# A decoder layer on one core: feed-forward weights prepared in the last pairs of the self-attention, the cross attention's end in halves and pairs of tiles

## The reference

```python
x = layernorm(x + self_attention(x))     # 16 heads of 64, rotary, causal
x = layernorm(x + cross_attention(x))    # 16 heads of 16, 5 samples a query
x = layernorm(x + feed_forward(x))       # 704 hidden units, fake quantisation
```

## Time and profile before

| engine | busy us | share |
|---|---|---|
| TensorE, matmuls | 1846.8 | 88% |
| VectorE | 1521.4 | 72% |
| GpSimd | 1496.5 | 71% |
| ScalarE | 1316.2 | 62% |

### The profile page before, as it was taken

The page is one execution under the profiler, slowest core; times in us unless marked ns, Lnnn a source line. Parts: engine busy times, 40 slices in busy tenths (PEclk is TensorE's granted clock), DMA queues, the critical chain, the costliest instruction groups (busy, mean ns, idle before and its releaser), DMA issues. The chain is left out here.

```text
span 2110.7 us, 43268 instructions
## 1 busy us (share of the span) xinstructions
PE 1846.8 (88%) x17255; PEld 1127.7 (53%) x17259; DVE 1521.4 (72%) x2147; ACT 1316.2 (62%) x1802; POOL 1496.5 (71%) x1122
## 2 busy tenths in 40 slices
PE   5889999999999999999999999588889898884475
PEld 3545455555555555555455454466677677663333
DVE  6857867868878868878768764257667676777787
ACT  3546656656556656666656655057887877874287
POOL 0767868878868878868778777168768797757256
PEclk8989999999999999999999999679999999997698
DMA  7022122122132032132032020200000000100002
GB/s 226 27 51 66 46 71 66 40 57 66 41 76 66 16 81 66 26 91 66 17 81 66 16 66 27 62 7 8 3 2 8 2 2 2 46 2 2 2 1 80
DMA packets 57511, 92.39 MB, mean 44 GB/s; under 512 B 25312, under 2 KB 35552, under 8 KB 53344
## 3 DMA queue, kind: packets, MB, share of 16 engines
q1 hardware_dynamic: 48096, 89.36, 16.4%
q10 hardware_dynamic: 9216, 0.27, 0.2%
HBM read 51.33 MB, written 4.46 MB: 26 GB/s over the span
## 5 line engine op out<-in xcount | busy, mean ns | idle before, releaser
L947 POOL TENSOR_TENSOR acc<-acc,probs 128x1024 f32<-128x1024 f32 (+3 forms) x320 | 583.0, 1822 | 105.9 <-ACT probs L650 75.4
L650 ACT ACTIVATE probs<-psum 128x1024 f32<-128x1024 f32 (+3 forms) x384 | 290.7, 812 | 162.7 <-PE psum L501 160.7
L594 ACT ACTIVATE chunks<-psum 128x1024 bf16<-128x1024 f32 x288 | 282.0, 1026 | 123.7 <-PE psum L460 78.0
L493 PE MATMUL psum<-operands 64*128 64x512 f32 (+3 forms) x1536 | 309.9, 515 | 17.4 <-ACT chunks L594 16.9
L1523 ACT ACTIVATE onehot<-psum 128x1024 bf16<-128x1024 f32 x320 | 324.5, 1045 | 0.0
L801 DVE TENSOR_REDUCE lows<-chunks 128x2 f32<-128x1024 bf16 (+1 forms) x224 | 266.7, 1217 | 73.4 <-ACT chunks L594 63.5
L517 PE MATMUL psum<-probs,vals 128*64 128x512 f32 (+3 forms) x1536 | 296.1, 503 | 22.5 <-POOL probs L926 12.0
L1353 PE MATMUL psum<-pieces,onehot 128*128 128x64 bf16 x7680 | 281.6, 197 | 14.3 <-ACT vs L1530 13.0
L1353 PEld LDWEIGHTS psum<-pieces,onehot 128*128 128x128 bf16 x7680 | 262.8, 101 | 47.8 <-issue 24.6
L926 POOL TENSOR_SCALAR_AFFINE_SELECT probs<-probs 128x256 f32<-128x256 f32 x256 | 149.2, 600 | 127.5 <-ACT probs L650 127.5
L1994 POOL TENSOR_TENSOR vs<-vs,wgt 128x1280 f32<-128x1280 f32 x64 | 151.9, 2373 | 107.1 <-DVE wgt L1770 102.4
(11 more groups left out here) (243 smaller groups left out, 3397.9 us busy)
## 6 DMA issues: line engine op xcount, KB each, us to landing
operands<-turned SPq DMA_DIRECT2D x124, 256.0 KB, 5.1
rden<-inverse_rows SPq DMA_DIRECT2D x64, 256.0 KB, 3.9
raw<-in_wqk SPq DMA_DIRECT2D x30, 256.0 KB, 4.3
y<-in_x SPq DMA_DIRECT2D x1, 4096.0 KB, 17.9
wo<-in_wo SPq DMA_DIRECT2D x16, 256.0 KB, 2.6
out<-res SPq DMA_DIRECT2D x16, 256.0 KB, 2.1
raw<-in_wv SPq DMA_DIRECT2D x15, 256.0 KB, 4.3
raw<-in_xT SPq DMA_DIRECT2D x12, 256.0 KB, 4.0
```

The costliest lines, as they stand in the source:

```text
L493: nc.tensor.matmul(dst[:, hh, 0:width], ops[n % OBUF][rows, 1, kt * P:(kt + 1) * P].bitcast(F32), ops[n % OBUF][rows, 0, a:a + width].bitc ...
L594: nc.scalar.activation(chunks[k % MBUF][:, :, :], slot("max", n, c)[:, :, :], ACT.Copy, scale=-1.0)\
L650: nc.scalar.activation(probs[u % PBUF][:, :, 0:width], slot("s", n, u)[:, :, 0:width], ACT.Exp, scale=1.0 / D ** 0.5).then_inc(s_exp, 1)
L947: G.tensor_tensor(dst, dst, src, ALU.add).then_inc(s_acc, 1)
```

## The change

It does four things.
1. SyncE loads the raw weights of the feed-forward near the end of the self-attention, into the room of the projection's buffers. In pairs 29 to 31 VectorE takes scales (`PREPARE_AT`) and clips, ScalarE does the scaling (`SCALE_AT`), TensorE transposes in three otherwise empty full slots (`TURN_WEIGHTS_AT`), ScalarE copies. The quantising and the transposes after the last head are removed, and with them the transposed row of w_down's scales; the feed-forward reads the column by DMA instead.
2. In the cross attention the softmax is split in two parts, after the multiplies of units 0 and 1 of the same head, `weights` comes after the multiply of unit 0, and `exps` after unit 2. The last round's softmax is done in two halves of two heads, the first inside heads 62 and 63. GpSimd normalises batch 2 before it weighs round 14, and it leaves head 63's values to VectorE (`weigh_last`).
3. The end works on pairs of tiles: the transposes and copies of the first half of the context ride in heads 13 and 14 of the last batch, the projections with this half are made ahead for six tiles, then transposes, copy, projection, residual and statistics go by pairs, deviations and normalising by halves. The maxima of y are taken batch by batch (`TOP_AT`, `largest`), the last ones here and not in the feed-forward.
4. In the second pair of the self-attention, one `turn` of GpSimd comes after the first masks and additions of that pair.

```diff
+WEIGHTS = 3
+TURN_WEIGHTS_AT = {(PAIRS - 2, 3): 0, (PAIRS - 1, 1): 1, (PAIRS - 1, 3): 2}
+PREPARE_AT = {(PAIRS - 3, 5): [("scales", 0)], (PAIRS - 2, 0): [("scales", 1)], (PAIRS - 2, 2): [("clip", 0)],
+              (PAIRS - 2, 3): [("scales", 2)], (PAIRS - 2, 5): [("clip", 1)], (PAIRS - 1, 1): [("clip", 2)]}
+SCALE_AT = {(PAIRS - 2, 1): 0, (PAIRS - 2, 4): 1, (PAIRS - 1, 0): 2}
...
+    full = ("w", TURN_WEIGHTS_AT[n, m], 0) if (n, m) in TURN_WEIGHTS_AT else full_at(n, m)
...
+            def load_weights():
+                sp.wait_ge(s_split, len(pieces))
+                sp.wait_ge(s_qk_done, QK_UNITS * GROUPS)
...
+                if i == GROUPS - 2:
+                    load_weights()
...
+            def turn_weights(n):
...
+                pe.wait_ge(s_whq, n + 1)
+                wait_slot(pe, "w", n, 0)
...
+            def scale_weights(n):
+                act.wait_ge(s_set, 8)
+                act.wait_ge(s_winv, n + 1)
+                for t in range(IT if n < 2 else KT):
+                    last = nc.scalar.activation(weights.raw[n][:, t, :], weights.raw[n][:, t, :], ACT.Identity,
+                                                bias=magic[:, 0:1], scale=hidden.winv[n][:, t:t + 1])
+                last.then_inc(s_wsc, 1)
...
+            def copy_weights(n):
+                act.wait_ge(s_wht, n + 1)
+                src = slot("w", n, 0).bitcast(BF16)
+                if n < 2:
+                    nc.scalar.activation(hidden.wT[n][:, :, :], src[:, :, 0:INNER], ACT.Copy).then_inc(s_whc, 1)
...
+            def weight_scales(n):
+                wscale, winv = hidden.wscale[n], hidden.winv[n]
+                dve.wait_ge(s_wraw[n], 16 * (3 if n < 2 else 1))
+                V.tensor_reduce(wscale[:, :], weights.raw[n][:, :, :], AX.X, ALU.max, apply_absolute_value=True)\
+                 .then_inc(s_wscale, 1)
+                dve.wait_ge(s_wscale, 2 * n + 1)
+                V.tensor_scalar(wscale[:, :], wscale[:, :], 1.0 / QMAX, None, ALU.mult).then_inc(s_wscale, 1)
+                dve.wait_ge(s_wscale, 2 * n + 2)
+                V.reciprocal(winv[:, :], wscale[:, :]).then_inc(s_winv, 1)
+            def clip_weights(n):
+                dve.wait_ge(s_wsc, n + 1)
+                V.tensor_scalar(weights.quantised[n][:, :, :], whole(weights.raw[n][:, :, :]), QMAX, -QMAX - 1.0,
+                                ALU.min, ALU.max).then_inc(s_whq, 1)
...
-                    if full and full[0] == "qk" and (n or m != LAST_CHUNKS):
+                    elif n == 1 and m == 0:
+                        turn(1, QK_UNITS - 1)
+                    elif full and full[0] == "qk" and (n or m != LAST_CHUNKS):
                         turn(full[1], full[2])
...
+LATE_RIDERS_AT = {(13, 1): ("cT", 0), (13, 3): ("cT", 1), (14, 1): ("cT", 2), (14, 3): ("cT", 3)}
+TOP_AT = {(LATE - 1, 5, 1): 0, (LATE, 10, 0): 1}
...
+            def late_turn(tp):
+                pe.wait_ge(s_c2, NHG * XB)
+                if tp >= 2:
+                    pe.wait_ge(s_c2T, count("cT", LATE, TILE_PAIRS + tp - 2))
+                for t in range(2):
+                    last = nc.tensor.transpose(turn_banks[tp % 2][:, t, :], ctx2[:, 2 * tp + t, (KT - 1) * P:], ident[:, :])
+                last.then_inc(s_c2t, 1)
+            def late_out(t, kt):
+                return nc.tensor.matmul(late[t], outT[:, kt, t * P:(t + 1) * P], wo[:, kt, :],
+                                        start=kt == 0, stop=kt == KT - 1)
+            def late_project(tp):
+                pe.wait_ge(s_c2T, count("cT", LATE, TILE_PAIRS + tp))
+                if 2 * tp >= len(early):
+                    pe.wait_ge(s_done, RIDERS["out"] * LATE + 1)
+                for t in (2 * tp, 2 * tp + 1):
+                    if t >= len(early):
+                        late_out(t, 0)
+                    last = late_out(t, 1)
+                last.then_inc(s_wo, 1)
...
+                    if u == EXPS_AT and j == SOFT_AT and r:
+                        exps(r - 1)
+                    if u == EXPS_AT and n == HEADS_ALL - LAST:
+                        exps(ROUNDS - 1)
+            exps(ROUNDS)
+            for tp in range(TILE_PAIRS):
+                copy_late(tp)
...
+            def late_residual(tp):
+                dve.wait_ge(s_x1b, BIAS_PARTS * XB)
+                dve.wait_ge(s_wo, RIDERS["out"] * LATE + tp + 1)
+                src = psum[:, 2 * tp:2 * tp + 2, 0:E] if 2 * tp < len(early) else psum[:, 0:2, E:2 * E]
+                pair = y[:, LATE * TT + 2 * tp:LATE * TT + 2 * tp + 2, :]
+                V.tensor_tensor(pair, src, pair, ALU.add).then_inc(s_done, 1)
+                dve.wait_ge(s_done, RIDERS["out"] * LATE + tp + 1)
...
+            def weigh_last():
+                j = HG - 1
+                dve.wait_ge(s_vc, UNITS * HEADS_ALL)
+                dve.wait_ge(s_w, len(turns))
+                both = vs[:, (ROUNDS - 1) % 2, j, :, :]
+                v = both.rearrange("p t (k d) -> p (t k) d", d=HD)
+                w = wgt[:, j * TT:(j + 1) * TT, :, :].rearrange("p t k c -> p (t k c)").unsqueeze(2)
+                V.tensor_tensor(v, v, w.broadcast_to([P, TT * NK * 2, HD]), ALU.mult).then_inc(s_wl, 1)
+                dve.wait_ge(s_wl, 1)
+                V.tensor_reduce(ctx2[:, :, (H - 1) * HD:H * HD], both.rearrange("p t (k d) -> p t d k", d=HD), AX.X, ALU.add)
             def gather(r, j):
...
+                    x = ROUNDS - 1 if n >= HEADS_ALL - LAST else r - 1
+                    first = LAST if n >= HEADS_ALL - LAST else SOFT_AT
+                    if x >= 0 and (j, u) == (first, 0):
+                        softmax_scores(x)
+                    if x >= 0 and (j, u) == (first, 1):
+                        softmax_max(x)
+                    if x >= 0 and (j, u) == (first + 1, 0):
+                        weights(x)
                     between(b, h, u)
...
-            softmax(ROUNDS - 1)
-            weights(ROUNDS - 1)
-            dve.wait_ge(s_sam, UNITS * HEADS_ALL)
-            for n, first in enumerate((0, 1, 3)):
-                quantise(n)
-                for j in range(first, (1, 3, HG)[n]):
-                    gather(ROUNDS - 1, j)
+            softmax_scores(ROUNDS)
+            softmax_max(ROUNDS)
+            weights(ROUNDS)
+            gather(ROUNDS - 2, HG - 1)
+            for j in range(LAST):
+                gather(ROUNDS - 1, j)
+            weigh_last()
+            gather(ROUNDS - 1, LAST)
             dve.wait_ge(s_x2, XB - 1)
-            st.then(V.tensor_reduce(hidden.ytop[:, 0:1], y[:, 0:(XB - 1) * TT, :], AX.XY, ALU.max,
-                                    apply_absolute_value=True))
-            for t in range(TT):
-                residual(XB - 1, t)
-                if t % 4 == 3:
-                    x2_statistics(XB - 1, range(t - 3, t + 1))
-            aggregate(1, s_var2)
-            x2_normalise(XB - 1, range(TT))
+            largest(XB - 2, (XB - 2) * TT, (XB - 1) * TT)
+            for tp in range(TILE_PAIRS):
+                late_residual(tp)
+                statistics(LATE, range(2 * tp, 2 * tp + 2))
+                if tp % 2:
+                    aggregate(1, s_var2, range(2 * tp - 2, 2 * tp + 2))
+            for half in range(2):
+                x2_normalise(half)
+                first = LATE * TT + TT // 2 * half
+                largest(LATE + half, first, first + TT // 2)
             st.settle()
         @block.gpsimd
@@ -1958,11 +2130,11 @@
                 pool.wait_ge(s_dev1, 1)
                 G.tensor_tensor(rstd[0][:, :], rstd[0][:, :], power[:, :], ALU.pow).then_inc(s_std1, 1)
-            def x2_deviations(b):
-                pool.wait_ge(s_var2, b + 1)
...
+                if b == LATE:
+                    x2_deviations(b - 1)
+                    x2_normalise(b - 1)
                 weigh_values(NHG * b + 2)
-                if b:
+                if 0 < b < LATE:
                     x2_deviations(b - 1)
                     x2_normalise(b - 1)
             weigh_values(ROUNDS - 1)
-            x2_deviations(XB - 1)
+            weigh_values(ROUNDS, HG - 1)
+            for half in range(2):
+                x2_deviations(LATE + half, slice(TT // 2 * half, TT // 2 * (half + 1)))
```

320 lines of the change are left out of this document (184 added, 136 removed).

## The result

The changed kernel takes 2099.33 us (median of 20 runs, 2092.98 to 2103.79) against 2109.28 for the kernel before (20 runs, 2100.65 to 2113.27): a ratio of 0.9955, 95% interval 0.9945 to 0.9966. That is some 9.5 us less, where 27.4 were forecast. The profiled execution has a span of 2097.8 us, 12.9 less than before.

A forecast was written before the change was run, and what follows sets the result against it. In the cross-attention loop TensorE or ScalarE is nearly always at work; its end runs through VectorE and GpSimd. -27.7 - 10.4 + 9 + 1.7 = -27.4, so 2112.4 became 2085.0 us, range 2071 to 2100.

The forecast's parts named there:

- half softmax: Heads 62 and 63 of the cross attention: the last softmax's first half there makes VectorE's loop end 1.4 us later.
- part 4: Second self-attention pair: one rotary turn of GpSimd goes behind the first masks, delaying operands and chunk: +1.7 us (-1 to +4).
- Part 1: End of the cross attention: GpSimd normalises earlier, head 63 on VectorE, tail by pairs: -27.7 us (-24 to -31).
- Part 2: Cross-attention loop: softmax in pieces removes TensorE stalls, less maxima and transposes: -10.4 us (-18 to +1).
- the 14 us: Cross-attention loop: 14 of 17.6 us of TensorE's waits for copies of values taken as gone (0 to 20).
- Rival A: Cross-attention loop gains nothing; pieces only shift the late multiply from slot 0 to slot 1: 2099 us, chance 0.14.
- it keeps all its work, so nothing beyond the stalls: Cross-attention loop: ScalarE, busy almost all of a plain head, comes next, so only the stalls are gained.
- the two signs of failure: Wait for copies of values staying above 10 us, or transposes waiting more than 5 us for the clips.
- the six stretched scalings of 1948.41: End of the old cross attention: VectorE's weight scalings, 8.32 us, 1.39 each, read as contention with GpSimd.
- head 63's multiplication: End of the cross attention, on VectorE: 1.9 us; waiting for or holding GpSimd would make it 2.4 us later.
- Part 3: Last self-attention pairs: preparing the feed-forward weights there queues ScalarE, VectorE and TensorE: about +9 us (4 to 17).
- The start of the feed-forward: TensorE's first instruction waits for the clips' DMA, 3.5 us after the block began; that wait stays.

The follow-up runs named there:

- run 1: Changed kernel with the old softmax order in rounds 0 to 14 (both pieces ahead of the first multiply, exponential at the head's end): 2101.0 us, ratio 0.9940.
- run 9: Changed kernel, softmax still in two pieces, only the exponential moved behind the head's fourth copy of values instead of the third: 2095.7 us, ratio 0.9918.
- run 10: Kernel before, with only the softmax of rounds 0 to 14 in four pieces, one behind each multiply: 2092.6 us, ratio 0.9911.
- run 7: Changed kernel with ScalarE's six scalings of the gate weights one step later in the last but one pair: 2096.8 us, ratio 0.9928.
- run 3: Changed kernel with the last round's softmax whole and after the loop, instead of a half in heads 62 and 63: 2096.0 us, ratio 0.9928.
- run 6: Changed kernel with GpSimd's bias additions to the next batch's queries after it has weighed round 4b+2 instead of before: 2097.1 us, ratio 0.9934.
- run 8: Changed kernel with the feed-forward's constants (identities, clips) there before its block begins: 2094.5 us, ratio 0.9919.
- run 5: Changed kernel with the softmax of rounds 0 to 14 in four pieces, one behind each multiply, exponential after the fourth copy: 2081.3 us, ratio 0.9857.
- run 11: Changed kernel with four softmax pieces in all rounds, the half round in heads 62 and 63 included, and the feed-forward's constants early: 2075.4 us, ratio 0.9831.
- run 12: Changed kernel with four softmax pieces, the feed-forward's constants early, and the last round's softmax whole behind the loop: 2072.1 us, ratio 0.9811.

## Why the forecast was off, step by step

In the traces the whole came to -12.9 us where -27.4 were forecast. The loop to head 60 gave +2.2 for -10.4, the end with its half softmax in heads 62 and 63 -21.2 for -27.7, the last pairs +9.2 for +9. The time before pair 29 was 4.8 us shorter (part 4 had +1.7) through the clock of that execution, the start of the feed-forward 1.3 longer, and 0.4 lie between the last pair and the first head.

**Part 1, the end: the tail nearly right, the half softmax wrong.** From the last head to the block 58.3 us became 31.2, 27.1 less, where the terms behind the last head come to 29. The term of -27.7 had also 1.4 us in it for the half softmax inside heads 62 and 63; these heads and head 61 became 5.9 us longer, so the term as it was put is -21.2, outside its own range of -24 to -31. Some sizes inside were wrong both ways, and the listed terms add up to 1943.7 for the heads out, not to 1944.4. I had the context ready 14.4 us after the last head (1944.4 against 1928.6 + 1.4) and it took 14.9; the way there was another. VectorE's second half of the softmax and its weights cost 5.7 us, not 2.6, since two of its operations were held; its multiplication 2.04 (I took 1.9), its sum 2.29 (2.5). The 14.2 us behind it were 15.8 to the end of VectorE's last instruction. GpSimd waited 1.45 and 2.13 us for weights which I had on time. Heads out came at 1956.4 instead of 1944.4 mostly because everything ahead was later.

**Part 2, the loop: this step failed.** "The delay for each multiply is then below the 1.3 us in which TensorE samples the other slot": it was up to 2.6 us where both operations of the first piece were held, and in 8 of 15 rounds at least one of them was (0.74 to 1.64 us instead of 0.32). I had the hold before me (753 ns against a third of a microsecond) and read its mean over all rounds as a price for each, where it is up to a full GpSimd instruction in half of the rounds and nothing in the others. What the runs showed in place of the 14 us: 3.3 us for the pieces with the exponential's new place (run 1), some 5 by the times for the pieces alone (run 9 against run 1, 13.6 between their traces), neither clear of the noise, and 19 for one operation a gap (run 10). Rival A had the mechanism, "from slot 0 to slot 1", at 0.14; its 2099 is the time that came, by luck: its sum had -27.7 at the end, where -21.2 came, and +3.6 for the loop, where nothing came that can be told from zero. Where nothing was held, the forecast holds in part: head 60 took 6.40 us for the 6.5 stated, after 7.34, and heads 16, 32 and 48 lost 0.8 to 1.0 us too, but heads 40, 52 and 56 were 0.2 to 1.0 us longer than before. The second miss was "it keeps all its work, so nothing beyond the stalls": the exponential moved into the middle of the head cost 2 to 8 of the 15 to 21 us between the changed kernel's loop and the four pieces (ratios 0.9955 or, in run 7, 0.9928; then 0.9918 and 0.9857). The stalls gained by small pieces then brought the clock with them: 24 us in run 10's trace, 19 in its times, against the 14 that I took and the 20 that I put as the end. Of the two signs of failure that I had named neither came (7.4 us for the copies of values, 1.2 for the clip): the lateness had moved to a wait that I was not watching, TensorE's for one-hots.

**The half softmax in heads 62 and 63: 5.9 us instead of 1.4.** This is the miss inside part 1. It comes from part 1's own gain: GpSimd, having normalised first, weighs round 14 from 1920 to 1936, which is when these operations now run. The edit made its own contention (run 3).

**The Trainium skill** (SBUF — State Buffer, section "Who interferes with whom") says that a vector instruction with two SBUF inputs contends with a GpSimd one that reads SBUF. The traces agree in the main: 0.32 us each with GpSimd idle (runs 3 and 6), 0.7 to 1.6 in the changed kernel's held rounds, up to 2.1 beside the weighing; but not with every GpSimd instruction, as said below. The prediction called the six stretched scalings of 1948.41 a sign of the same rule; they have one tensor input, and for such instructions the prediction left out that the same section of the Trainium skill excepts the 2-port modes. I applied the rule to head 63's multiplication and to the weights, where GpSimd stood waiting, and not to the scores in front of them.

**Part 3, the weights: right in sum, in part by luck**, +9.2 (pair 30 +8.0, pair 31 +1.2) for 9, with the waits of 3.3 us behind the scaling and 1.2 for the clip where 3.0 and 2.2 were put. The sum had no term for the clock: behind the wait of 3.3 us TensorE ran at a granted clock of 0.5, its eight scores took 3.79 us instead of 2.05, and the matmuls up to 1281.7 lost some 2.7 us so. Run 7 shows that the terms don't add: take the scaling's wait away, and other waits and the low clock make up for it. The same section of the Trainium skill says that a tensor_scalar in a 2-port mode contends with GpSimd too. The trace agrees as far as it goes: the clip, a tensor_scalar, took 2.70 us beside GpSimd's additions (3.03 in run 7) and 0.95 at 1294.17, where none was running; whether it ran in such a mode no row shows.

**Part 4, the moved turn: 0** for +1.7. The operands were issued at 108.27, as forecast, and their chunk began at 115.44, not 117.2: the data was there 7.2 us after the first issue, where I had 4.1 and 5 in a row.

**The start of the feed-forward** kept its wait, as stated (4.8 us in this trace, 3.5 before). It was cheap to remove (run 8).

## What to carry to other kernels

An operation that is slow on average in a profile is often a short one that is held in some places: list it place by place with what the other engine does there, before moving it. When work is put between the links of a tight chain, each link's slack is the measure, held operations at their held length; here one operation a gap cost little where two did not fit. And a gain that puts another engine to work earlier also moves that engine's interference onto whatever now runs beside it.

## What the runs showed of the hardware

The granted clock made two fifths to a half of the loop's gain: with fewer stalls, TensorE's busy time for the same 8548 matmuls fell from 441.4 to 429.0 us (run 10, of 24.4 us) and from 444.7 to 437.4 (run 5, of 17.8). And executions of the same code differed through the clock alone: the loop of runs 11 and 12 is one program and took 479.8 and 485.8 us, with 49.3 and 50.0 of standing; the third pair took 39.0 to 41.7, head 20 with four pieces 9.4 to 12.0 us. A single trace can't price an edit of a few microseconds in such a loop. And not every GpSimd instruction holds a two-input one: beside its normalising (L2105, one instruction after another) the same operations took 0.32 to 0.36 us in three rounds of the changed kernel (at 1677, 1817 and 1913 us).
